# A gated attention block in Trainium2: the last stage's instructions in another order

## The reference

```python
x = x + tanh(g_xattn) * attention(layernorm(x), ctx, ctx)      # 16 heads of 8
n = layernorm(x)
# ffn(n): causal self-attention with rope, then a mixture of experts
a   = n + ctx @ out_proj_w.T + out_proj_b          # ctx: result of the attention
x1  = layer_norm(a, ln1_w, ln1_b)
gates = softmax(x1 @ gate_w.T + gate_b)             # 8 experts
top_gates, top_idx = top_k(gates, 2)
moe = sum over the two chosen experts of top_gate * (x1 @ expert_w[e].T + expert_b[e])
out = x + tanh(g_ffn) * layer_norm(x1 + moe, ln2_w, ln2_b)
```

## Time and profile before

| | |
|---|---|
| median of 3 runs | 441.24 us (440.28 to 442.39) |
| the profiled execution's own time | 441.23 us |
| its span in the profile | 439.4 us |
| last stage, full steps | 339 to 418 us, in steps of equal length |
| DVE busy, PE busy, ACT busy, POOL busy between 360 and 380 us | 18.72, 19.38, 16.28, 17.21 us of 20 |
| TensorE clock granted in all of that | 1.00 |

### The profile page before, as it was taken

The page is one execution under the profiler, slowest core; times in us unless marked ns, Lnnn a source line. Parts: engine busy times, 40 slices in busy tenths (PEclk is TensorE's granted clock), DMA queues, the critical chain, the costliest instruction groups (busy, mean ns, idle before and its releaser), DMA issues.

```text
span 439.4 us, 17671 instructions
## 1 busy us (share of the span) xinstructions
PE 385.7 (88%) x6538; PEld 231.3 (53%) x6538; DVE 369.2 (84%) x1188; ACT 288.4 (66%) x728; POOL 323.3 (74%) x740
## 2 busy tenths in 40 slices
PE   0368888888888899999999999999999999999994
PEld 0134544454444555666666666666655555555541
DVE  6587999999997878888878878877848999999987
ACT  1126777767766766666666666666665788788772
POOL 4456767767778988888888788849823788888884
PEclk9999999999999999999999999999999999999999
DMA  6855686685553333333434343333000000000001
GB/s 163 193 155 160 170 199 169 162 180 145 132 158 101 98 100 105 104 106 104 109 106 125 103 127 100 99 105 96 12 4 2 1 25 13 24 27 12 25 25 48
DMA packets 88037, 42.76 MB, mean 97 GB/s; under 512 B 16000, under 2 KB 87824, under 8 KB 87952
## 3 DMA queue, kind: packets, MB, share of 16 engines
q1 hardware_dynamic: 80864, 39.59, 34.2%
q10 hardware_dynamic: 7088, 2.04, 2.0%
HBM read 5.69 MB, written 2.10 MB: 18 GB/s over the span
## 4 chain that ended last, share of the span: by engine, by line
PE 41%; DVE 6%; ACT 5%; issue 3%; POOL 1%; SPq 1%; DMA 1%; POOLq 0%; ACTq 0%; DVEq 0%
PE s_bank L923 6%; PE u_bank L499 6%; PE st_bank L923 6%; PE s_bank L421 4%; PE s_bank L434 3%; DVE r L697 2%; PE t_bank L413 2%; PE u_bank L944 2%; PE u_bank L942 2%; PE u_bank L909 2%; PE t_bank L407 2%; ACT z_x_t L1018 2%; ACT part L577 1%; PE u_bank L514 1%; PE t_bank L408 1%
## 5 line engine op out<-in xcount | busy, mean ns | idle before, releaser
L716 DVE TENSOR_REDUCE nm<-s_bank 128x4 f32<-128x512 f32 x256 | 171.5, 683 | 36.3 <-PE s_bank L434 34.0
L599 ACT ACTIVATE pt<-st_bank 128x512 f32<-128x512 f32 x250 | 147.5, 602 | 74.0 <-PE st_bank L434 51.6
L434 PE MATMUL s_bank<-qk 64*64 64x128 bf16 (+1 forms) x1584 | 103.5, 220 | 12.1 <-DVE nm L716 5.7
L499 PE MATMUL u_bank<-pt,vaug 128*32 128x128 f32 x2048 | 108.3, 286 | 1.6 <-DVE ao L733 0.2
L434 PE MATMUL st_bank<-qk 64*64 64x128 bf16 (+1 forms) x1540 | 98.2, 218 | 0.0
L434 PEld LDWEIGHTS s_bank<-qk 64*64 64x64 bf16 (+1 forms) x1584 | 73.8, 104 | 36.1 <-issue 18.9
L434 PEld LDWEIGHTS st_bank<-qk 64*64 64x64 bf16 (+1 forms) x1540 | 69.1, 103 | 0.0
L499 PEld LDWEIGHTS u_bank<-pt,vaug 128*32 128x32 f32 x2048 | 41.1, 108 | 27.5 <-issue 5.2
L421 PE MATMUL s_bank<-mqk,idb 64*64 64x256 bf16 x256 | 38.3, 292 | 0.8 <-ACT pt L599 0.4
L327 POOL TENSOR_TENSOR part<-r,part 128x512 bf16<-128x512 f32 x32 | 37.1, 1158 | 1.4
L421 PE MATMUL st_bank<-mkq,idb 64*64 64x256 bf16 x244 | 35.7, 293 | 0.0
(11 more groups left out here) (136 smaller groups left out, 815.4 us busy)
## 6 DMA issues: line engine op xcount, KB each, us to landing
qk<-part SPq DMA_DIRECT2D x221, 128.0 KB, 2.8
x_all<-x SPq DMA_DIRECT2D x16, 128.0 KB, 2.6
qk<-qrow SPq DMA_DIRECT2D x32, 64.0 KB, 2.0
c_all<-ctx_in SPq DMA_DIRECT2D x14, 128.0 KB, 2.8
out<-z_o SPq DMA_DIRECT2D x14, 128.0 KB, 1.8
qk<-mts ACTq DMA_DIRECT2D x34, 32.0 KB, 2.7
qk<-mts SPq DMA_DIRECT2D x30, 32.0 KB, 2.1
ewt<-exp_t SPq DMA_DIRECT2D x1, 512.0 KB
```

Source lines behind the costliest of these rows:

```text
L434: ins = pe.matmul(to[outs, :], fixed[:, outs], moving, start=not masked, stop=True, skip_group_check=masked)
L499: ins = pe.matmul(u_bank[b][32 * j:32 * j + 32, r * P:(r + 1) * P], v, pt[m % 4][:, j, :], start=half == 0, stop=half == 1, skip_group_che ...
L599: act.activation(pt[m % 4][:, :, :].rearrange("k j q -> k (j q)"), transposed_bank(m)[:, :], ACT.Exp).then_inc(ex, 1)
L716: dve.tensor_reduce(nm[q % 2][:, first:first + HEADS], s_bank[n % 2][:, :].rearrange("q (j k) -> q j k", j=HEADS), AX_X, ALU.max, negate=T ...
```

## The change

The same instructions run, the same number on each engine, on the same data. Their order in the last stage is another:

- DVE: `gating` of pair s-2 comes first, and `gated_pairs` and `gated_sum` of pair s-3 behind it. Before, the first stood ahead of it and the second in its midst. `shift_logits` is cut in two: the bias is added behind the two large additions, and the maximum is taken between the two sorts of statistics; both one step earlier in the list.
- ACT: the eight gatings of a pair are cut into four and four, with the exponentials of the next pair between them, and a signal behind each four. `normalise2` and `normalise1` stand at the step's end; `normalise1` of pair s is followed by `copy_att` of pair s+1.
- PE: `transpose_n` comes between the bias product and the product that adds the gated sum.

```diff
@@ PE
-                    else:
-                        pe.wait_ge(z_yg, g)
-                for b in range(G):
+                for b in range(G):
+                    if gc >= 1 and k == 1:
+                        pe.wait_ge(z_yg, (g - 1) * G + b + 1)
...
-            def gated_sum(g, gc):
+            def sum_of_biases(g, gc):
...
+
+            def gated_sum(g, gc):
+                dst = u_bank[1][:, 0:W]
                 pe.wait_ge(z_yq, g + 1)
...
+                if in_z(c, 3) and s - 3 < LAST:
+                    sum_of_biases(s - 3, c - 3)
+                if in_z(c, 1) and s - 1 < LAST:
+                    transpose_n(s - 1, c - 1)
...
                 if in_z(c, 3) and s - 3 < LAST:
                     gated_sum(s - 3, c - 3)
-                if in_z(c, 2):
+                if in_z(c, 2) and s - 2 < LAST - 1:
                     gates_t(s - 2, c - 2)
@@ ACT
             def body(s, c):
-                if in_z(c, 2):
-                    gates_exp(s - 2, c - 2)
-                if in_z(c, 1):
-                    normalise1(s - 1, c - 1)
                 if in_z(c, 0):
                     copy_att(s, c)
-                if in_z(c, 4) and s - 4 < LAST - 1:
+                if in_z(c, 1):
+                    copy_x1(s - 1, c - 1)
+                if in_z(c, 4) and s - 2 == LAST:
                     normalise2(s - 4, c - 4)
                 if s - 2 == LAST:
                     gate_last_experts(s - 2, c - 2)
                 if in_z(c, 2):
                     copy_gates(s - 2, c - 2)
-                if in_z(c, 1):
-                    copy_x1(s - 1, c - 1)
                 if in_z(c, 2) and s - 2 < LAST:
-                    gate_experts(s - 2, c - 2)
+                    gate_experts(s - 2, c - 2, 0)
+                    gates_exp(s - 1, c - 1)
+                    gate_experts(s - 2, c - 2, 1)
+                if in_z(c, 4) and s - 2 < LAST:
+                    normalise2(s - 4, c - 4)
+                if in_z(c, 0):
+                    normalise1(s, c)
@@ DVE
             def body(s, c):
                 if in_z(c, 2):
-                    shift_logits(s - 2, c - 2)
+                    gating(s - 2, c - 2)
                 if in_z(c, 3) and s - 3 < LAST:
                     gated_pairs(s - 3, c - 3)
-                if in_z(c, 2):
-                    gating(s - 2, c - 2, (s - 3, c - 3) if s - 3 < LAST else None)
+                    gated_sum(s - 3, c - 3)
                 if in_z(c, 2):
                     experts(s - 2, c - 2)
                 if in_z(c, 0):
                     attention_add(s, c)
                     experts_add(s - 3, c - 3)
+                    add_gate_bias(s - 1, c - 1)
                     attention_stats(s, c)
+                    logit_maxima(s - 1, c - 1)
                     experts_stats(s - 3, c - 3)
```

More of the change, by code:

```diff
@@ L961, in body @@
                     transpose_att(s, c)
+                if s - 1 == LAST:
+                    transpose_n(s - 1, c - 1)
+                    gates_t(s - 2, c - 2)
+                if in_z(c, 3) and s - 3 < LAST:
+                    sum_of_biases(s - 3, c - 3)
+                if in_z(c, 1) and s - 1 < LAST:
+                    transpose_n(s - 1, c - 1)
+                if s - 2 == LAST:
+                    gates_t(s - 2, c - 2)
                 if in_z(c, 3) and s - 3 < LAST:
                     gated_sum(s - 3, c - 3)
-                if in_z(c, 2):
+                if in_z(c, 2) and s - 2 < LAST - 1:
                     gates_t(s - 2, c - 2)
-                    if s - 2 == LAST:
-                        last_gated_sum(s - 2, c - 2)
-                if in_z(c, 1):
-                    transpose_n(s - 1, c - 1)
+                if s - 2 == LAST:
+                    last_gated_sum(s - 2, c - 2)
                 if in_z(c, 0):
@@ L1056, in gate_experts @@
                     act.wait_ge(z_yp, g)
-                for b in range(G):
-                    for e in range(HALF):
-                        ins = act.activation(zyg[:, b, e, :], e_bank[b][1][:, e * P:(e + 1) * P], ACT.Copy,
-                                             scale=zg[i][:, b, HALF + e:HALF + e + 1])
+                for e in range(HALF):
+                    ins = act.activation(zyg[:, b, e, :], e_bank[b][1][:, e * P:(e + 1) * P], ACT.Copy,
+                                         scale=zg[i][:, b, HALF + e:HALF + e + 1])
                 ins.then_inc(z_yg, 1)
@@ L1104, in early @@
                     copy_gates(0, 0)
-                    gate_experts(0, 0)
+                    gate_experts(0, 0, 0)
+                    gate_experts(0, 0, 1)
             def steps():
+                gates_exp(1, 1)
+                normalise1(2, 2)
                 z_steps(body)
@@ L1153, in z_dve, with add_gate_bias @@
             per_seq = [P, G, NE]
-            def shift_logits(g, gc):
+            def add_gate_bias(g, gc):
                 k = g * GATE
@@ L1159, in shift_logits, with logit_maxima, gating @@
                                   gbb[:, :].unsqueeze(1).broadcast_to(per_seq), ALU.add).then_inc(z_gate, 1)
+            def logit_maxima(g, gc):
+                k = g * GATE
                 dve.wait_ge(z_gate, k + 1)
                 dve.tensor_reduce(zm[:, :], zl[:, :, :], AX_X, ALU.max, negate=True).then_inc(z_gate, 1)
-            def gating(g, gc, second_level=None):
+            def shift_logits(g, gc):
+                add_gate_bias(g, gc)
+                logit_maxima(g, gc)
+            def gating(g, gc):
                 i = gc % 2
@@ L1178, in gating @@
                     dve.match_replace(zq[:, b, :], z8[:, b, :], zp[:, b, :], 0.0).then_inc(z_gate, 1)
-                if second_level is not None:
-                    gated_sum(*second_level)
                 dve.wait_ge(z_gate, k + 9)
@@ L1204, in gated_pairs @@
             def gated_pairs(g, gc):
-                dve.wait_ge(z_yg, g + 1)
+                dve.wait_ge(z_yg, (g + 1) * G)
                 if gc >= 1:
@@ L1277, in body @@
                     experts_moments(s - 3, c - 3)
-                elif in_z(c, 3):
-                    all_experts(s - 3, c - 3)
-                if in_z(c, 3):
+                else:
+                    if s - 1 == LAST:
+                        shift_logits(s - 1, c - 1)
+                    if in_z(c, 3):
+                        all_experts(s - 3, c - 3)
                     if s - 3 == LAST - 1:
@@ L1304, in steps @@
                 attention_sum(2, 2)
+                shift_logits(1, 1)
                 z_steps(body)
```

5 lines of the change are left out of this document (2 added, 3 removed).

## The result

The changed kernel takes 446.81 us (446.26 to 447.08, 4 runs), the kernel before in the same session 441.48 us: a ratio of 1.012 (95% interval 1.010 to 1.014), slower by 1.2%. The profiled execution took 446.26 us, 1.8 us more than its span, as before. The forecast was 446.0, range 439.5 to 448.0, slower with chance 0.77.

What follows compares the result with a forecast made beforehand. No engine was idle enough; the 6.60 us last-stage step, paid twelve times, bounds the kernel, set by two waits. 441.2 + 5.2 (steps of 7.03) + 0.1 (entry) - 0.5 (drain) = 446.0 us, range 439.5 to 448.0.

Steps and rivals of the forecast that it cites:

- A: Start of DVE's attention addition (L1126) in a last-stage step, taken as zero; the next was forecast at A + 7.03.
- E: End of the attention's moments (z_mv) on DVE in a step, forecast at A + 1.83; before the change A + 1.68.
- pairs first: DVE's pairs' addition starts at E + 1.14, 0.03 before POOL's two offsets at E + 1.17, and keeps them out.
- first offset getting ahead: Rival: POOL's first offset precedes the pairs; about 441 (chance 0.11), or 443.5 with every second step 7.03 (chance 0.10).
- The holds: DVE's two-SBUF-input additions keep POOL out 0.54 (pairs) and 0.30 (sum); offsets end at E + 2.42, 0.75 later.
- whole instruction: Skill's rule that the hold lasts the entire DVE instruction; by it the step would be 7.15, time near 447.3.
- The chain: Offsets, z_n, attention copy (ends E + 3.63), transpose (E + 3.69), projection, next A: step 7.03 instead of 6.60.
- no meeting: Rival: offsets and pairs do not meet, or meet without a price; step 6.28, time 437.0, chance 0.12.
- The lost 0.37: PE between projection and logits: wait for ACT's uncovered copy of z_n's transpose, some 0.37, removed by the earlier transpose.
- The sum: Forecast total: 441.2 + 5.2 (12 x 0.43) + 0.1 - 0.5 = 446.0 us.
- Entry: First full step's transpose waits for a copy behind z_n: about +0.1.
- Drain: Last pair's logits waited 0.75 for their copy; the earlier transpose takes part away, taken as 0.5 gained.

Runs made afterwards that it cites:

- run 3: Changed kernel with the pairs' addition on half its data, half the gated experts left out of the output: 442.04 us in one run.
- run 2: Changed kernel with the pairs' addition and the sum replaced by one reduction over four gated experts: 445.07 us against 440.50, ratio 1.010.
- run 5: As run 2, but the reduction sums only two of the four gated experts, the others left out: 436.44 us against 441.09, ratio 0.990.
- run 4: Changed kernel with ACT's copy of the next attention output ahead of the normalisation that makes z_n: 447.38 us in one run.
- run 1: Changed kernel with the first two of eight expert products moved between gating and pairs' addition on DVE: 445.66 us against 440.50, ratio 1.012.
- run 6: Changed kernel with the first norm's offsets computed by ACT instead of POOL, normalise2 behind copy_att: 445.66 us against 441.09, ratio 1.011.
- run 11: As run 1, with the second experts' products between the pairs' addition and the sum: 445.18 us against 441.14, ratio 1.009.
- run 12: Run 6 with pairs' addition amid the gating, sum behind it, and ACT's second normalisation cut in two: 437.46 us against 441.35, ratio 0.993.
- run 8: Kernel before with only DVE's part of the change, pairs' addition and sum behind the gating: 445.51 us in one run.
- run 9: Run 1 without POOL's multiplication by the second norm's weights: 438.36 us against 441.14, ratio 0.994.
- run 7: Kernel before with only PE's early transpose of z_n, ACT copying it before the gates: 446.85 us in one run.

## Why the prediction was right, step by step

- **The moments end at A + 1.83.** Measured 368.38 + 0.23 - 366.76 = 1.85. From there the pairs start at E + 1.12 (forecast 1.14) and the offsets are issued at E + 1.20 (1.17). The margin is 0.08, not 0.03. A part of that is what the forecast named when it weighed the first offset's getting ahead: POOL is late by what it was kept out. Its z_o ends at 368.65, behind E at 368.61, so z_ve starts at E + 0.12 and not 0.09. The order "pairs first" on which the forecast hung was right in all twelve steps, so the rival of the first offset getting ahead did not occur.
- **The holds.** The offsets took 1.20, forecast 2.42 - 1.17 = 1.25. The last ends at E + 2.40 (2.42). The hold by width was right: with the pairs half as wide (run 3) the offsets take 0.27 less, where 0.28 was expected, and the two reductions, runs 2 and 5, remove it. This is "SBUF — State Buffer", section "SBUF: two separate sides", of the Trainium skill as far as who excludes whom goes; its "whole instruction" is more than the trace shows: the second offset would have been held up to the sum's end at 370.88 and have ended 0.27 later, at 371.15 at the earliest, where it ended at 371.01. (By that rule the forecast's own sum is 12 x 0.55 - 0.4 on 441.2, so 447.4, not 447.3.)
- **The chain.** z_n 0.03 behind the offsets; copy's end at E + 3.57 (3.63); transpose at E + 3.72 (3.69); from there to the next A 1.43 (1.51), so A + 7.00 (7.03). PE followed the copy by 0.15, not 0.06, and what stands between transpose and addition took 0.08 less: these two misses nearly cancel. Run 4 shows that the order of copy and z_n within this chain is worth nothing. Run 5 shows that without the hold the step is 6.32. The rival "no meeting" had 6.28 from the chain alone; it left out that PE itself is busy 6.32.
- **The lost 0.37.** This reading was too large. In the changed kernel nothing is waited for ahead of the logits, and they start 0.61 behind the projection (373.12 to 373.73) where it was 0.82. So 0.21 was lost, which is what the bracket of the earlier trace rows says. The forecast's sum does not use the 0.37.
- **The sum.** Steps 12 x 0.40 = 4.8 (5.2). *Entry*, forecast +0.1: the first step took 6.29 instead of 6.13, which is right, but the stage began 0.66 earlier (its first attention addition at 332.48, before at 333.14). Over the runs this point lies anywhere between 332.3 and 333.5, also where the queues ahead are the same, so I put it down to scatter. *Drain*, forecast -0.5: this term had the wrong sign. The logits' wait for their copy of 0.75 is indeed gone. But the last pair's offsets are held like all others, so the logits start 6.85 behind the last addition instead of 6.64, and what follows took another 0.6 longer for a reason below. -0.66 and +0.16 + 4.76 + 0.84 make the span's 5.1. That the profiled 446.26 lies so close to 446.0 is in part luck: the steps gave 0.4 less than forecast and the stage began 0.66 earlier for no known reason, while the drain cost 1.3 more than forecast.
- **What I had not seen.** The forecast treated the meeting as one place. Runs 1, 6 and 11 show that it is a matter of the whole queue: held at one place or another, POOL hands it on. My expectations for runs 1 and 6, which freed only the first offsets, were wrong by some 6 us for that reason, and run 2's by the reduction's price.

A single POOL instruction for both offsets was not tried.

## What to carry to other kernels

When an order is changed, list for DVE and POOL what will lie beside what, and give each two-input addition a place under work of the other engine that nobody waits for; here the new order would have made the step 0.28 shorter (run 5), and the meeting made it 0.4 longer. Look at the slack of the held engine's whole queue and at who stands behind each wait on the third engine: freeing one victim only moves the hold to the next one in the queue (runs 1, 6). A fix is done when the engine with the greatest load shows no waits (run 12), not when the first wait is gone.

## What the runs showed of the hardware

- **The price of a reduction.** Summing four tiles with a stride took 1.92 us for 128x1024 inputs, summing two took 0.69 for 128x512. I had expected about 1.2 for the first; two additions took 0.68 and 0.43.
- **The hold works both ways.** In run 1 at the stage's beginning POOL's wide multiplication began just behind the pairs' addition (336.59) and took 1.22 where it takes 0.73. DVE's sum, which came while it ran, took 0.83 where it takes 0.42:

```profile
336.63 1.22 POOL L1339 TENSOR_TENSOR z_nw<-z_n,l1w 128x256 f32<-128x256 f32 x1 [1.00 <-ACT z_n L1045]
337.30 0.83 DVE L1236 TENSOR_TENSOR z_gated_sum<-z_gated_pairs 128x256 f32<-128x256 f32 x1
```

- **An addition with one input in PSUM holds nothing.** m_bank and u_bank are PSUM tiles. In every full step of the changed kernel the two additions that read them, as wide as the sum, lie beside POOL's wide instructions, and neither side is longer than alone (0.42 and 0.41, 0.72 and 0.73). The sum, with both inputs in SBUF, is the same operation at the same width: compare the two rows above.

```profile
366.43 0.72 POOL L1342 TENSOR_TENSOR z_x<-z_nw,l1b 128x256 f32<-128x256 f32 x1
366.76 0.42 DVE L1141 TENSOR_TENSOR z_h<-m_bank,xn_all 128x256 f32<-128x256 f32 x1 [0.82 <-PE m_bank L886]
367.11 0.41 DVE L1245 TENSOR_TENSOR z_x_moe<-u_bank,z_acc 128x256 f32<-128x256 f32 x1
367.11 0.73 POOL L1350 TENSOR_TENSOR z_yw<-z_y,l2w 128x256 f32<-128x256 f32 x1
```

- **Once begun, a small POOL instruction runs on.** In run 8 the factor starts 0.06 ahead of the pairs and takes its 0.71; in run 9 it starts 0.20 behind them (368.75) and takes 1.04.

```profile
370.12 0.71 POOL L798 TENSOR_TENSOR z_rstd<-z_ve,mhalf 128x2 f32<-128x2 f32 x1
370.18 0.69 DVE L1208 TENSOR_TENSOR z_gated_pairs<-z_gated 128x512 f32<-128x512 f32 x1
```

- **The clock fell in the drain.** In the changed kernel's windows behind the full steps the granted clock (third column from the right) is half, so 1.2 in place of 2.4 GHz, from 430 into the next window:

```profile
430.00:432.00 2.00, 2.00 (x5) 0.97 (x5) 1.71 (x12) 1.56 (x8) 1.73 (x4) 0.50 0.00 0
432.00:434.00 2.00, 2.00 (x5) 0.82 (x4) 1.90 (x10) 0.88 (x3) 1.82 (x5) 0.66 0.22 66
```
```profile
430.00 3.63 PE L923 MATMUL s_bank<-ewt,z_x_t 128*128 128x512 f32 x4
```

The four products took 3.63 instead of 1.96, with 1.12 us of PE's idle time ahead of them at 427.97. They took 1.67 longer by that, of which no more than 0.6 shows in the drain's 0.84. Runs 4 and 7 show the same dip near 431 to 435. Runs 6 and 8, with steps of 6.9, do not, and the kernel before has its dip only behind PE's last product. So I can't say what brings it about.
